# Two transformer blocks on one core: a layer norm inside the second FFN moved behind its matmul, the front reordered, and zero matmuls at two places

## The chip, the cores and the metric

The program runs on one core of one Trainium2 chip, in one launch. The metric is the device time of an execution in microseconds (us). Three runs of the kernel before gave 410.98, 412.43 and 413.91 us, median 412.43.

The names of the engines are those of the profile: PE is TensorE (PEld its weight loads), DVE is VectorE, ACT is ScalarE, POOL is GpSimd, SP is SyncE, which here only issues DMAs. Each engine works through its own list of instructions in order; semaphores tie the lists together.

## The reference

The input x has 4 batches of 256 tokens with 256 features, in float32. Two blocks follow each other; both add an attention and a feed-forward network (FFN) of the same normed input to x:

```python
x = L0_attn_seq
xn = _layernorm(x, axis=-1)
x = x + _L0_attn_ref(xn, ...) + _L0_ffn_ref(xn, ...)
xn = _layernorm(x, axis=-1)
x = x + _L1_attn_ref(xn, ...) + _L1_ffn_ref(xn, ...)
```

The first attention reshapes its input into many sequences of only two tokens; a causal mask lets a token see so little that the attention comes down to a choice between two learned memory entries. The first FFN is one ternary matrix 256 by 256. The second attention has 32 query heads and 4 key/value heads of width 64, rotary position embedding on q and k, and a causal softmax over 256 tokens. The second FFN is the part that the change rebuilds:

```python
def ternarize_weights(w):
    gamma = jnp.mean(jnp.abs(w))
    return jnp.sign(jnp.round(w / (gamma + EPS))) * gamma
def bitlinear(x, w):
    xn = layer_norm(x)
    ...
    return jnp.einsum('bsd,od->bso', x_hat, w_hat)
h = bitlinear(x, w_fc)                    # 256 -> 1024
h = jax.nn.gelu(h, approximate=False)
return bitlinear(h, w_proj)               # 1024 -> 256, with a layer norm of h inside
```

## The kernel before, in words

Everything is written out by hand: one function for each engine (`@block.tensor`, `@block.vector`, and so on) holds that engine's list in program order, and every wait is explicit. Products in nearly full float32 accuracy are made by splitting a matrix into a high part and a low part ("hi", made by ACT or DVE while rounding, and "lo", the difference, made by DVE or POOL) and adding the matmuls of the parts.

**The front.** SP issues the loads from HBM. PE multiplies the memory entries with the first attention's weights (`g_products` L972, `m_products` L980, four pieces each), transposes the normed tokens y0 (L962), forms the scores of the first attention (L1010) into one bank, DVE and ACT turn them into shares of two (`small`, L754 to L767), and PE multiplies (`ffn_0` L1029, `attention_0` L1036). DVE adds the result to x for one batch after another (`add0` L783), takes the statistics of the next norm (`stats1`), asks POOL for the square root (POOL raises to the power -0.5, `root` L574), writes the normed tokens y1 (`norm1` L323, called `y` in the trace), and PE transposes them (`turn_tokens`), from which ACT makes xT_hi (L465) and DVE xT_lo (L812). The ternary weights are made on DVE in three passes over each matrix (`ternary`, L735 to L737).

**The second FFN** runs in 8 tiles of 128 tokens, in STEPS that PE walks at L1267 and the others beside it. For a tile t: `fc` (L1081, PE), `gelu` (L484, ACT), `hidden_stats` (L826 to L832, DVE), a root on POOL, `hidden_factors` (L836, L837, DVE), `hidden_y` (L497, ACT, one pass over 1024 columns that applies the inner layer norm), `hidden_T` (L962, PE, two halves of four transposes), `hidden_hi` (L491, ACT), `hidden_lo` (L841, DVE), `proj` (L1109, PE, 16 matmuls), `ffn_add` (L846, DVE). Tile t is transposed and multiplied three and four steps after its `fc`.

**Fills and blocks.** Between these steps PE projects q, k and v of the second attention ("fills", L1139 and L1155). A fill of q or k is a block n = 0, 1, 2, ...; five fills are prepared in the front (k of batch 0, q of group 0 in two halves, v of batch 0, first half of q of group 1). ACT copies a block out of PSUM (`raw`, L477), SP moves its halves with four DMAs (`turned`, L359 and L360), POOL multiplies and adds the rotary embedding in five passes (L621, L623, L631, L632, L633), and SP moves the result into qT with four DMAs or kT with eight (L380, L383). `raw` and `turned` have two buffers: ACT may copy block n only when POOL is through with `rope_products` of block n-2, and waits for that in its list. POOL also makes the low parts of the weights of q and of the output (L588), two after each of the first blocks, 18 units in all.

**The second attention** is 16 pairs (batch, group) of 6 units, so 96 slots n. In slot n PE computes the scores (L1191, mask L1194), transposes the probabilities of slot n-2 (L962), multiplies with v (L1228) and projects out (L1248); DVE and ACT do the softmax. The fills go on in the slots: in an iteration (6 slots) the second half of q of the next pair at unit 0, the first half of q of the pair after it at unit 3, and at units 4 k or v of the next batch. The first half of a pair's q is needed at its unit 0, the second half at its unit 3. So block 9, the second half of q of pair 3, is projected in slot 12 and needed in slot 21.

## Time and profile before

| | |
|---|---|
| Median of three runs | 412.43 us |
| Profiled execution, time of it | 411.61 us |
| Profiled execution, span | 409.8 us |
| PE busy | 369.4 us, 90% of the span |
| DVE, ACT, POOL busy | 310.9, 251.9, 272.2 us |
| HBM read | 13.14 MB |

The profiled execution's own time is 1.8 us above its span, and 0.8 us below the median. The profile's strip of 40 slices (10.2 us each) shows PE at nine tenths or more from slice 13 to the last but one; all its holes lie in the first 12 slices, the front. POOL is at nine tenths in slices 14 to 18, and mostly lower later. In the kernel's timelines idle time stands in brackets behind an instruction, with the instruction that ended it.

### The profile page before, as it was taken

The page shows a single profiled execution, that of the slowest core. Times are in us where ns is not written, and L with a number is a line of the kernel's source. Part 1 is how long each engine was busy: PE and PEld are TensorE (multiplying, and loading weights), DVE is VectorE, ACT ScalarE, POOL GpSimd, SP SyncE. Part 2 cuts the span into 40 slices and gives each one's busy share as a digit, 9 for nine tenths or more (in the row PEclk, how much of TensorE's full clock was granted, in tenths as well). Part 3 has the DMA queues.
Part 4 walks back from the last instruction along what each step waited for, and adds up shares of the span by engine and source line. Part 5 has one row for each costly group of instructions (what it writes and reads, how often), then busy time and mean ns, then how long its engine had stood idle before and what let it go on. Part 6 is the DMA issues. An engine that isn't in the chain of part 4 may idle for free.

```text
span 409.8 us, 8388 instructions
## 1 busy us (share of the span) xinstructions
PE 369.4 (90%) x2860; PEld 344.7 (84%) x2860; DVE 310.9 (76%) x693; ACT 251.9 (61%) x803; POOL 272.2 (66%) x225
## 2 busy tenths in 40 slices
PE   3968593399889999999999999999999999999995
PEld 1645582379879999999999999999999999998985
DVE  3776786876768777877877788787778778787883
ACT  1142354267768877575767767586776767677671
POOL 3350437346597999998776989767698886777000
PEclk9986798599999999999999999999999999999999
...
GB/s 262 417 417 189 0 26 27 103 26 53 78 78 41 115 97 87 136 130 97 99 108 86 101 168 119 92 95 111 87 104 166 118 95 90 111 80 93 78 0 27
DMA packets 34219, 45.15 MB, mean 110 GB/s; under 512 B 5505, under 2 KB 25986, under 8 KB 33794
## 3 DMA queue, kind: packets, MB, share of 16 engines
...
q14 instruction: 18, 0.15, 0.1%
q10 hardware_dynamic: 146, 0.00, 0.0%
HBM read 13.14 MB, written 1.05 MB: 35 GB/s over the span
## 4 chain that ended last, share of the span: by engine, by line
PE 78%; DVE 9%; ACT 6%; POOL 2%; issue 2%; DMA 2%; SPq 0%; DVEq 0%; POOLq 0%
PE bank L1228 17%; PE bank L1191 13%; PE bank L962 12%; PE bank L1139 12%; PE bank L1248 11%; PE bank L1194 3%; PE bank L1109 2%; DMA wq0T<-in_L_attn_w_qkv_dram 2%; PE bank L980 2%; PE bank L1155 1%; PE bank L972 1%; PE bank L1081 1%; DVE hT_lo L841 1%; POOL qkvT_lo L588 1%; DVE y L323 1%
## 5 line engine op out<-in xcount | busy, mean ns | idle before, releaser
L507 ACT ACTIVATE bank<-bank,neg_max 128x256 f32<-128x256 f32 (+1 forms) x256 | 101.2, 396 | 6.7 <-DVE neg_max L869 6.6
L516 ACT ACTIVATE probT_hi<-bank 128x512 fp32r<-128x512 f32 x96 | 57.5, 599 | 73.3 <-PE bank L962 73.1
L869 DVE TENSOR_REDUCE neg_max<-bank 128x2 f32<-128x512 f32 (+1 forms) x96 | 66.0, 687 | 32.5 <-PE bank L1194 32.4
L1228 PE MATMUL bank<-probT_hi,v 128*128 128x256 f32 x384 | 76.6, 296 | 0.5 <-DVE oT_lo L897 0.5
L623 POOL TENSOR_TENSOR rope_b<-turned,cst 128x512 f32<-128x512 f32 x36 | 46.7, 1297 | 40.0 <-DMA turned<-raw 39.8
L1191 PE MATMUL bank<-kT,qT 128*128 128x256 f32 (+1 forms) x512 | 73.2, 275 | 0.0
L885 DVE TENSOR_TENSOR prob<-bank,rsum 128x512 f32<-128x512 f32 x96 | 66.3, 691 | 3.3
L1191 PEld LDWEIGHTS bank<-kT,qT 128*128 128x128 f32 x512 | 66.6, 192 | 0.0
L891 DVE TENSOR_TENSOR probT_lo<-bank,probT_hi 128x512 fp32r<-128x512 f32 x96 | 65.2, 680 | 0.5 <-ACT probT_hi L516 0.4
L1228 PEld LDWEIGHTS bank<-probT_hi,v 128*128 128x128 f32 x384 | 58.8, 190 | 3.2 <-issue 1.9
L962 PE MATMUL bank<-cst,prob 128*128 128x128 f32 x384 | 57.8, 273 | 1.4 <-DVE prob L885 1.4
L1228 PE MATMUL bank<-probT_lo,v 128*128 128x256 f32 x192 | 54.1, 282 | 0.0
L507 ACT ACTIVATION_READ_ACCUMULATOR bank<-bank,neg_max 128x1 f32 x256 | 53.6, 209 | 0.0
L962 PEld LDWEIGHTS bank<-cst,prob 128*128 128x128 f32 x384 | 45.9, 141 | 4.2 <-DVE prob L885 1.8
L633 POOL TENSOR_TENSOR split_lo<-rope_a,split_hi 128x512 fp32r<-128x512 f32 x36 | 46.2, 1285 | 2.8
L631 POOL TENSOR_TENSOR split_hi<-rope_a,rope_b 128x512 fp32r<-128x512 f32 x36 | 46.3, 1286 | 2.5
L621 POOL TENSOR_TENSOR rope_a<-raw,cst 128x512 f32<-128x512 f32 x36 | 46.9, 1302 | 0.0
L632 POOL TENSOR_TENSOR rope_a<-rope_a,rope_b 128x512 f32<-128x512 f32 x36 | 46.5, 1291 | 0.0
L897 DVE TENSOR_TENSOR oT_lo<-bank,oT_hi 128x256 fp32r<-128x256 f32 x64 | 27.1, 424 | 18.4 <-ACT oT_hi L521 18.1
L1228 PEld LDWEIGHTS bank<-probT_lo,v 128*128 128x128 f32 x192 | 36.5, 190 | 0.0
L1139 PE MATMUL bank<-xT_hi,qkvT_hi 128*128 128x256 f32 x144 | 30.8, 295 | 0.0
L1194 PE MATMUL bank<-mask_b,ident_b 128*128 128x256 bf16 (+1 forms) x96 | 30.6, 318 | 0.0
...
## 6 DMA issues: line engine op xcount, KB each, us to landing
...
qT<-split_hi SPq DMA_DIRECT2D x64, 128.0 KB, 2.4
qT<-split_lo SPq DMA_DIRECT2D x64, 128.0 KB, 2.4
...
kT<-split_hi SPq DMA_DIRECT2D x16, 128.0 KB, 2.4
```

Of the source, the lines that this page charges most:

```text
L507: ins = nc.scalar.activation(own, own, ACT.Exp, bias=neg_max[it % 2][:, first + j:first + j + 1], accum_out=sums[it % 2][:, first + j:firs ...
L516: nc.scalar.activation(probT[0][:, n % 4, :], bank[2 + n % 2][:, :], ACT.Copy).then_inc(t_hi, 1)
L621: pool.tensor_tensor(a, whole, cos, ALU.mult)
L623: own_done(pool.tensor_tensor(z, half, sin, ALU.mult))
L632: own_done(pool.tensor_tensor(a, a, z, ALU.add))
L869: dve.tensor_reduce(neg_max[n // UNITS % 2][:, unit_columns(n % UNITS)], score_bank(n)[:, :].rearrange("p (h k) -> p h k", h=heads), AX.X, ...
L885: dve.tensor_tensor(a, e, share, ALU.mult).then_inc(s_norm, 1)
L891: dve.tensor_tensor(lo, bank[2 + n % 2][:, :], hi.bitcast(F32), ALU.subtract).then_inc(t_lo, 1)
L962: ins = pe.transpose(ps[:, P * j:P * j + P], a, ident)
L1139: ins = pe.matmul(bank[place][:, SEQ * j:SEQ * j + SEQ], qkvT[w][:, k, at:at + P], xT[s][:, k, SEQ * b:SEQ * b + SEQ], start=i == 0, stop= ...
L1191: pe.matmul(ps[:, keys * j:keys * j + keys], qT[it % 2][:, h + j, P * c:P * c + P], kT[b % 2][:, g, s, 0:keys], start=j == 0 and s == 0, s ...
L1228: ins = pe.matmul(group_bank(), v[b % 2][:, DH * z:DH * z + P], p, start=m == 0, stop=m == last)
```

## The change

The names keep their meaning; line numbers in the diff's headers are left out.

- **The inner norm is deferred.** `hidden_y` is gone. PE transposes the gelu's output as it is, and `proj` multiplies it. `ffn_add` multiplies the product by the tile's factor while it adds (one DVE instruction as before). The mean's part, mean times factor times the column sums of the weights, is added on POOL: `mean_part`, two instructions of 128x256 a tile, placed after the weights' low parts that follow blocks 4 to 11. The column sums are eight matmuls on PE in step 5 (`column_sums`), copied out by ACT. `add_out` waits for the mean parts.
- **The pipeline is shorter.** Tile t is transposed one step after its `fc` and multiplied two steps after. STEPS falls from 12 to 10, and slots 0 and 1 alone are placed in the steps. All fills go to bank 6, the hidden transposes to banks 4 and 7. Fill k of batch 0 now waits until all four batches are added to x.
- **Ternary weights** take one pass on DVE (`rounded`) and one on ACT (`sign`).
- **y1** is written by ACT (`normal1`), with a bias for which POOL makes one more small product after each root.
- **The front's order.** The load of the constants goes behind x, that of w_fc ahead of `wout`. PE transposes y0 before the first `m_products`; the first score product's work on DVE no longer stands behind the sum over w_fc and the four casts of xT_hi; the constants' casts go from DVE to POOL.
- **Zero matmuls.** PE multiplies a zeroed bf16 tile 14 times into bank 5 at its start and 8 times into bank 4 ahead of `turn_tokens(0)`, 512 columns each; nothing reads the result.

```diff
-        SLOTS_AT = {8: (0,), 9: (1,), 10: (2,), 11: (3,)}
+        WCOL_STEP = 5
+        SLOTS_AT = {8: (0,), 9: (1,)}
         FILL = ([f for step in sorted(FILLS_IN) for f in FILLS_IN[step]]
                 + [f for it in range(ITS) for u in range(UNITS) for f in fills_at(it, u)])
         PREPARED = sum(map(len, FILLS_IN.values()))
...
+                    sp.dma_start(cst[:, 0:C_QC], const[:, 0:C_QC]).then_inc(ld["cst"], 16)
             sp.dma_start(nat_ffn0[:, :, :], w_ffn0).then_inc(ld["ffn0"], 16)
+            sp.dma_start(nat_fc[:, :, :], w_fc).then_inc(ld["fc"], 16)
             for i in range(WQ0_PIECES):
                 own = slice(piece * i, piece * i + piece)
                 sp.dma_start(wout0[:, own, :], w_out0[:, own, :]).then_inc(ld_wout[i], 16)
-            sp.dma_start(nat_fc[:, :, :], w_fc).then_inc(ld["fc"], 16)
...
+            def sign(n, w, out, done):
+
+                act.wait_ge(tern_in, n + 1)
+                nc.scalar.activation(out, w, ACT.Sign, bias=neg_magic[:, 0:1]).then_inc(done, 1)
...
-            for b in range(B):
-                whole_x(b)
+            whole_x(0)
+            whole_x(1)
+            whole_x(2)
             act.wait_ge(e_in, 1)
             nc.scalar.activation(small[:, 1, :], small[:, 0, :], ACT.Exp).then_inc(e_out, 1)
+            whole_x(3)
+            sign(0, nat_ffn0[:, :, :], ffn0T[:, :, :], tern0)
...
+            sign(1, nat_fc[:, :, :], fcT[:, :, :], tern_fc)
...
+                act.wait_ge(nb_done, b + 1)
+                for t in (2 * b, 2 * b + 1):
+                    ins = nc.scalar.activation(y1[:, b, t % 2, :], x[:, b, t % 2, :], ACT.Identity, bias=tok[:, 3, t:t + 1],
+                                               scale=tok[:, 0, t:t + 1])
+                ins.then_inc(y1_done, 1)
...
+            normal1(0)
             tokens_hi(0)
+            normal1(1)
             done = 3
             for step in range(STEPS):
-                hidden_hi(step - 3, 0)
-                if 0 <= step - 2 < TILES:
-                    hidden_y(step - 2)
-                hidden_hi(step - 3, 1)
+                hidden_hi(step - 1, 0)
+                hidden_hi(step - 1, 1)
                 if step < TILES:
                     gelu(step)
+                if step < B - 1:
+                    tokens_hi(step + 1)
+                empty(FILLS_IN.get(step, ()))
+                if step < B - 2:
+                    normal1(step + 2)
+                if step == 1:
+                    sign(2, nat_proj[:, :, :], projT[:, :, :], tern_proj)
                 if step == TILES - 1:
                     nc.scalar.activation(table_use[:, 0:1], table_use[:, 1:2], ACT.Exp)
-                if step in (0, 2, 3):
...
+                own = slice(2 * b, 2 * b + 2)
+                root(tok[:, 0:2, own], b + 3)
+                pool.wait_ge(root_out, b + 3)
+                pool.tensor_tensor(tok[:, 3, own], tok[:, 3, own], tok[:, 0, own], ALU.mult).then_inc(nb_done, 1)
...
+            def mean_part(t):
+
+                if t == 0:
+                    pool.wait_ge(wcol_done, 1)
+                pool.wait_ge(f_add, t + 1)
+                pool.tensor_tensor(mcol[:, :], wcol[:, :], ffac[:, t, 4:5].to_broadcast([P, DIM]), ALU.mult).then_inc(mean_made, 1)
+                pool.wait_ge(mean_made, t + 1)
+                part = x[:, t // 2, t % 2, :]
+                pool.tensor_tensor(part, part, mcol[:, :], ALU.add).then_inc(f_mean, 1)
+                pool.wait_ge(f_mean, t + 1)
...
+                if n - 4 < TILES:
+                    mean_part(n - 4)
...
-            def ternary(w, out, inverse):
-
-                link(dve.tensor_scalar(w, w, inverse, 1.0, ALU.mult, ALU.min))
-                link(dve.tensor_scalar(w, w, -1.0, MAGIC, ALU.max, ALU.add))
-                return dve.tensor_scalar(out, w, -MAGIC, None, ALU.add)
...
+            def rounded(w, inverse):
+
+                dve.tensor_scalar(w, w, inverse, MAGIC, ALU.mult, ALU.add).then_inc(tern_in, 1)
...
+            def high_part(b):
+
+                dve.wait_ge(full_done, b + 1)
+                dve.tensor_copy(xT[0][:, :, SEQ * b:SEQ * b + SEQ],
+                                yT_full[:, b, :].rearrange("p (k t) -> p k t", k=KC)).then_inc(x_hi, 1)
+
+            dve.wait_ge(sum_out, 2)
+            link(dve.tensor_scalar(winv[:, 0:1], bank[5][:, 0:1], 1.0 / (DIM * DIM), 1e-5, ALU.mult, ALU.add))
+            link(dve.reciprocal(winv[:, 0:1], winv[:, 0:1]))
+            rounded(nat_ffn0[:, :, :], winv[:, 0:1])
+            high_part(0)
...
+            for b in range(1, B):
+                high_part(b)
...
-            normal1(0)
             stats1(1)
+            hidden_scale(0)
             tokens_lo(0)
+            dve.wait_ge(sum_out, 3)
+            weight_scale(2, bank[3][:, 0:1]).then_inc(scaled, 1)
+            dve.wait_ge(scaled, 1)
...
             def ffn_add(t):
                 dve.wait_ge(f_out, t + 1)
-                dve.tensor_tensor(x[:, t // 2, t % 2, :], x[:, t // 2, t % 2, :], bank[5][:, 0:DIM],
-                                  ALU.add).then_inc(f_add, 1)
+                part = x[:, t // 2, t % 2, :]
+                dve.scalar_tensor_tensor(part, bank[5][:, 0:DIM], ffac[:, t, 3:4], part, ALU.mult, ALU.add).then_inc(f_add, 1)
...
+                dve.wait_ge(f_mean, 2 * b + 2)
...
-            weight_scale(2, bank[3][:, 0:1]).then_inc(scaled, 1)
             add0(2)
-            normal1(1)
             stats1(2)
+            tokens_lo(1)
             add0(3)
-            tokens_lo(1)
+            stats1(3)
+            rounded(nat_proj[:, :, :], winv[:, 2:3])
+            hidden_scale(1)
             for step in range(1, STEPS):
-                t = step - 3
-                if 0 <= t < TILES:
+                t = step - 1
+                if t < TILES:
+                    hidden_stats(t)
                     hidden_lo(t, 0)
-                if step <= TILES:
...
-                    normal1(3)
-                    ternary(nat_proj[:, :, :], projT[:, :, :], winv[:, 2:3]).then_inc(tern_proj, 1)
-                if step == 3:
-                    tokens_lo(3)
-                if 0 <= t < TILES:
                     hidden_lo(t, 1)
...
+
+                for _ in range(count):
+                    pe.matmul(bank[b][:, :], idle_in[:, 0:P], idle_in[:, :], start=True, stop=True)
+
+            pe.wait_ge(idle_ready, 1)
+            keep_busy(5, 14)
             pe.wait_ge(blk_done, 1)
             for i in range(WQ0_PIECES):
                 g_products(i)
-            m_products(0)
             for b in range(B):
...
-            m_products(1)
-            sum_up(0, bank[5][:, 0:1])
+            m_products(0)
             pe.wait_ge(g_done, 1)
...
+            sum_up(0, bank[5][:, 0:1])
+            sum_up(1, bank[5][:, 1:2])
+            m_products(1)
             m_products(2)
-            sum_up(1, bank[5][:, 1:2])
...
-            ffn_0(0)
             pe.wait_ge(prob0, 1)
             for b in range(B):
                 ins = pe.transpose(bank[4][0:2 * H, P * b:P * b + P], small[:, 3, 2 * H * b:2 * H * b + 2 * H], ident)
             ins.then_inc(p0_T, 1)
             m_products(3)
+            ffn_0(0)
             ffn_0(1)
...
             ffn_0(2)
             attention_0(2)
             sum_up(2, bank[3][:, 0:1])
+            keep_busy(4, 8)
             turn_tokens(0)
...
-                pe.wait_ge(f_y, t + 1)
...
+                pe.wait_ge(f_gelu, t + 1)
+                if t:
                     pe.wait_ge(f_lo, 2 * t + half - 1)
...
+            def column_sums():
+
+                emptied(pe, ("v", 0))
+                pe.wait_ge(tern_proj, 1)
+                pe.wait_ge(ones_done, 1)
+                for c in range(FF // P):
+                    ins = pe.matmul(bank[6][:, 0:DIM], ones_r[:, :], projT[:, c, :], start=c == 0, stop=c == FF // P - 1)
+                ins.then_inc(wcol_full, 1)
...
                 if f == ("k", 0):
-                    pe.wait_ge(y1_lo, 1)
-                if f == ("q", 0, 0):
                     pe.wait_ge(o0_added, B)
+                if f == ("q", 0, 1):
+                    pe.wait_ge(y1_lo, B)
+                if f == ("q", 1, 0):
+                    pe.wait_ge(wcol_done, 1)
...
-                t = step - 3
+                t = step - 1
                 if 0 <= t < TILES:
                     hidden_T(t, 0)
+                    hidden_T(t, 1)
                 if step < TILES:
                     fc(step)
-                if 0 <= t < TILES:
-                    hidden_T(t, 1)
+                if step < B - 1:
+                    turn_tokens(step + 1)
                 if t >= 1:
                     proj(t - 1)
-                if step in (0, 2, 3):
-                    turn_tokens(max(step, 1))
                 fill(FILLS_IN.get(step, ()))
+                if step == WCOL_STEP:
+                    column_sums()
```

What the change moves is seen in three places. On DVE early in the front, from the scale of w_ffn (`winv`) to the shares of the first attention (`small`), before:

```order
L735 TENSOR_SCALAR nat_ffn_107<-nat_ffn_107,winv 128x512
L736 TENSOR_SCALAR nat_ffn_107<-nat_ffn_107 128x512
L737 TENSOR_SCALAR ffn0T<-nat_ffn_107 128x512
L745 CAST xT_hi<-yT_full 128x2x256 x4
L748 TENSOR_REDUCE wsum<-nat_fc 128x1
L754 TENSOR_SCALAR small<-bank,tok 128x64 x4
L759 TENSOR_TENSOR small<-small 128x128
L761 TENSOR_TENSOR small<-small 128x128 x2
L764 TENSOR_TENSOR small<-small 128x128
L765 RECIPROCAL small<-small 128x128
L767 TENSOR_TENSOR small<-small 128x128 x2
```

and now:

```order
L788 TENSOR_TENSOR small<-small 128x128 x2
L798 TENSOR_SCALAR winv<-bank 128x1
L799 RECIPROCAL winv<-winv 128x1
L775 TENSOR_SCALAR nat_ffn_107<-nat_ffn_107,winv 128x512
L794 CAST xT_hi<-yT_full 128x2x256
L803 TENSOR_TENSOR small<-small 128x128
L804 RECIPROCAL small<-small 128x128
L806 TENSOR_TENSOR small<-small 128x128 x2
L794 CAST xT_hi<-yT_full 128x2x256 x3
L813 TENSOR_SCALAR wscale<-bank 128x1
L814 TENSOR_SCALAR winv<-wscale 128x1
```

The two further passes over `nat_ffn`, three of the four casts and the sum over `nat_fc` no longer stand ahead of `small`'s last instructions.

On DVE around the second tile's factors, before (`y` is the normed token of batch 3, `nat_proj` the ternary passes):

```order
L836 TENSOR_SCALAR ffac<-ffac,wscale 128x1
L837 TENSOR_SCALAR ffac<-ffac,fmv 128x1
L812 TENSOR_TENSOR xT_lo<-bank,xT_hi 128x256 x2
L323 TENSOR_SCALAR y_64<-x,mv,tok 128x256 x2
L801 RECIPROCAL tok<-tok 128x2
L802 TENSOR_TENSOR tok<-tok 128x2
L803 TENSOR_TENSOR tok<-tok 128x2
L804 TENSOR_SCALAR ffac<-tok,wscale 128x2
L735 TENSOR_SCALAR nat_proj<-nat_proj,winv 128x2048
L736 TENSOR_SCALAR nat_proj<-nat_proj 128x2048
L737 TENSOR_SCALAR projT<-nat_proj 128x2048
L841 TENSOR_TENSOR hT_lo<-bank,hT_hi 128x512
```

and now, for the first tile:

```order
L871 BN_AGGR fmv<-fstat 128x2
L720 TENSOR_SCALAR ffac<-fmv 128x1
L874 RECIPROCAL ffac<-fmv 128x1
L875 TENSOR_TENSOR ffac<-ffac,fmv 128x1
L884 TENSOR_TENSOR hT_lo<-bank,hT_hi 128x512 x2
L879 TENSOR_SCALAR ffac<-ffac,wscale 128x1
L880 TENSOR_SCALAR ffac<-ffac,fmv 128x1
L852 TENSOR_TENSOR xT_lo<-bank,xT_hi 128x256 x2
```

The low parts hT_lo of a tile now stand ahead of its factors L879, which wait for POOL's root; before, the first hT_lo stood behind the second tile's factors, the norm and the three passes.

On POOL from the weights' low parts after block 3, before:

```order
L588 TENSOR_TENSOR woT_lo<-nat_o,woT_hi 128x512
L621 TENSOR_TENSOR rope_a<-raw,cst 128x512
L623 TENSOR_TENSOR rope_b<-turned,cst 128x512
L631 TENSOR_TENSOR split_hi<-rope_a,rope_b 128x512
L632 TENSOR_TENSOR rope_a<-rope_a,rope_b 128x512
L633 TENSOR_TENSOR split_lo<-rope_a,split_hi 128x512
L588 TENSOR_TENSOR qkvT_lo<-nat_qkv,qkvT_hi 128x2x256
L588 TENSOR_TENSOR woT_lo<-nat_o,woT_hi 128x512
L621 TENSOR_TENSOR rope_a<-raw,cst 128x512
L623 TENSOR_TENSOR rope_b<-turned,cst 128x512
```

and now:

```order
L608 TENSOR_TENSOR woT_lo<-nat_o,woT_hi 128x512
L649 TENSOR_TENSOR rope_a<-raw,cst 128x512
L651 TENSOR_TENSOR rope_b<-turned,cst 128x512
L659 TENSOR_TENSOR split_hi<-rope_a,rope_b 128x512
L660 TENSOR_TENSOR rope_a<-rope_a,rope_b 128x512
L661 TENSOR_TENSOR split_lo<-rope_a,split_hi 128x512
L608 TENSOR_TENSOR qkvT_lo<-nat_qkv,qkvT_hi 128x2x256
L608 TENSOR_TENSOR woT_lo<-nat_o,woT_hi 128x512
L672 TENSOR_TENSOR mcol<-wcol,ffac 128x256
L675 TENSOR_TENSOR x<-x,mcol 128x256
L649 TENSOR_TENSOR rope_a<-raw,cst 128x512
L651 TENSOR_TENSOR rope_b<-turned,cst 128x512
```

Between two blocks there now stand two more instructions, the mean's part L672 and L675; this happens eight times.

## Rows read from the trace of the kernel before

**Rows 1.** Waits of PE, first 124.4 us: who waited for whom, us, times, longest.

```profile
PE bank L962 <- DVE hT_lo L841: 15.8, 6, 13.2
...
PE bank L962 <- DVE y L323: 4.8, 1, 4.8
...
PE bank L990 <- DVE wsum L748: 3.9, 1, 3.9
...
PE bank L972 <- DMA wq0T<-in_L_attn_w_qkv_dram: 7.3, 2, 7.0
```

**Rows 2.** Windows by stage: us, busy (x instructions) of each engine, granted clock, DMA share, GB/s.

```profile
78.00:124.40 46.40, 42.52 (x297) 38.72 (x298) 31.41 (x82) 31.63 (x61) 31.94 (x29) 0.94 0.25 58
...
124.40:172.30 47.90, 47.44 (x400) 46.15 (x400) 38.19 (x77) 35.58 (x123) 44.45 (x37) 1.00 0.41 97
...
172.30:409.80 237.50, 232.03 (x1940) 224.82 (x1938) 185.97 (x375) 159.43 (x571) 165.73 (x131) 1.00 0.41 98
```

**Rows 3.** Chain of waits, first 130 us: start us, us, what.

```profile
16.65 1.73 PE bank L980 x8
...
28.18 2.20 DVE wsum L748
...
34.35 1.06 PE bank L1052 x4
...
39.43 1.89 ACT abs_out L443 x2
...
41.34 1.28 ACT L533
...
43.43 2.49 POOL qkvT_lo L588 x2
...
45.92 0.98 POOL tok L574
```

**Rows 4.** Timeline of DVE: start us, us, instruction, [idle before, releaser].

```profile
41.07 0.69 DVE L783 TENSOR_TENSOR x<-x,bank 128x512 f32<-128x512 f32 x1 [2.48 <-PE bank L1036]
...
43.46 1.27 DVE L679 TENSOR_SCALAR tok<-tok 128x2 f32<-128x2 f32 x1
...
68.98 0.27 DVE L836 TENSOR_SCALAR ffac<-ffac,wscale 128x1 f32<-128x1 f32 x1 [3.17 <-POOL ffac L574]
...
70.08 2.74 DVE L323 TENSOR_SCALAR y<-x,mv,tok 128x256 f32<-128x256 f32 x2
```

**Rows 5.** Window of one of PE's waits.

```profile
43.80:48.60 4.80, 0.03 (x1) 0.00 (x0) 3.19 (x5) 0.60 (x2) 4.32 (x4) 0.70 0.00 0
```

**Rows 6.** Chain of waits, one tile of the hidden FFN and a fill.

```profile
94.69 0.63 PE bank L962 x4
...
99.53 1.46 PE bank L1139 x12
```

**Rows 7.** Timeline of POOL, the stage that follows.

```profile
111.94 1.27 POOL L631 TENSOR_TENSOR split_hi<-rope_a,rope_b 128x512 fp32r<-128x512 f32 x1
...
132.40 1.27 POOL L623 TENSOR_TENSOR rope_b<-turned,cst 128x512 f32<-128x512 f32 x1 [2.58 <-DMA turned<-raw]
...
172.30 1.29 POOL L621 TENSOR_TENSOR rope_a<-raw,cst 128x512 f32<-128x512 f32 x1
```

**Rows 8.** Timeline of ACT, block 5's copy out of PSUM.

```profile
127.81 0.62 ACT L477 ACTIVATE raw<-bank 128x512 f32<-128x512 f32 x1
```

**Rows 9.** POOL's groups by form: xcount, busy us, mean ns, idle before.

```profile
L633 POOL TENSOR_TENSOR split_lo<-rope_a,split_hi 128x512 fp32r<-128x512 f32 x36 | 46.2, 1285 | 2.8
...
L574 POOL TENSOR_TENSOR ffac<-ffac,neg_half 128x1 f32<-128x1 f32 x8 | 4.4, 550 | 19.6 <-DVE ffac L679 19.5
```

**Rows 10.** Timeline of SP's queue, block 9's last move.

```profile
175.03 0.61 SPq L380 DMA_DIRECT2D qT<-split_lo  x1
```

**Rows 11.** The page's DMA issues: KB each, median us from issue to landing.

```profile
qT<-split_lo SPq DMA_DIRECT2D x64, 128.0 KB, 2.4
```

**Rows 12.** Timeline of PE, scores of slot 21.

```profile
178.30 1.01 PE L1191 MATMUL bank<-kT,qT 128*128 128x128 f32 x8
```

125 lines of the change are left out of this document (53 added, 72 removed).

## Prediction

> **What bounds the kernel now.** I read the strip of 40 slices first: PE is at nine tenths from slice 13 on, with its holes in the front. PE's waits over the first 124.4 us come next: 13.2 us in one wait for hT_lo, 4.8 for y1, 3.9 for the sum over w_fc, 7.0 for the first weights [rows 1]. The windows by stage show the rest: from 124.4 us on PE is busy 279.5 of 285.4 us, at full clock [rows 2]. So from slot 3 on the kernel is PE's work; the change adds nothing to it there, and it can gain only by letting slot 3 start earlier. But the same windows show a second engine near its limit: POOL is busy 44.45 of the 47.9 us from 124.4 to 172.3. It stays behind its blocks there, and the change gives it more to do.
>
> **The front, replayed.** Times are the trace's, with durations of the same instructions.
>
> 1. PE's g products still end near 16.65 us, since the load of their second piece ends PE's wait. The y0 transposes then start at once; before, the first m products, 1.73 us, stood ahead [rows 3]. Transposes (2.3), one m piece (1.9) and the score product (1.9) put the scores at 22.8.
> 2. DVE before began `small` at 30.38, behind the sum over w_fc, though the scores were there at 24.6. From that to the shares on PE took 34.35-30.38 = 3.97 us [rows 3]. Now it starts at 22.8 with 0.85 us put in (scale, one pass, one cast): 27.6. Then the shares' transposes (0.53, half of the row's 1.06 at the lower clock), the m products (1.8), ffn_0 twice (0.95 each) and an attention product (0.87): the first add at 32.9 instead of 41.07 [rows 4], 8 us earlier.
> 3. ACT takes some of it back. The one pass over w_fc ends at 32.1; sign (1.9, priced like the pass L443 over the same 2048 columns), |w_proj| (2.1) and the table load (1.5) follow, then the first high part. POOL's first low part starts at 38.2 instead of 43.43. Behind it come low parts 2.49, root 0.98 [rows 3], the new small product (0.1 to 0.5, I take 0.3, by the nearest small POOL rows) and two norms on ACT (0.95): y1 is turned at 43.1 instead of 48.65, 5.5 us earlier.
> 4. The 8 zero matmuls ahead of it take 1.7 us while PE waits; PE is still idle for 4.9 us from 38.2 to 43.1. In the wait of 4.8 us before, the granted clock fell to a mean of 0.70 within the window, so to its lower level (1.2 GHz) [rows 5]. I let it fall again and price the pair of stretches alike. The 14 at the start lie inside PE's 7.0 us wait for weights: no cost, no gain, since the next piece is waited for anyway.
> 5. fc(0) starts at 47.0. Fill k now waits for all four adds, behind `tokens_lo(1)`: 52.4. PE idles 3.0 us there, a new wait. The second tile's transposes come at 59.7, proj(0) at 63.0 (before 86.1).
> 6. The 13.2 us wait arose on DVE: factors of tile 1 waited 3.17 us for POOL's root, then came the norm of batch 3 (2.74) and three ternary passes, 3.8 us, all ahead of hT_lo [rows 4]. POOL's root still stands behind a block's products, and DVE still waits for it, until 67.3; but both hT_lo of the tile now stand ahead. Only ffn_add(0) is late, and proj(1) with it: 1.5 us, at 69.5.
> 7. From there PE has no wait longer than a few tenths. A tile (two halves, fc, proj) takes 99.53-94.69 = 4.84 us, 0.19 of it from a start behind a wait, so 4.65; a fill 1.46 [rows 6]. Column sums are 8 matmuls of 0.12, 0.95 us, paid in full. Fill v ends at 79.0; two tiles, the sums and a fill later, q of block 3 ends at 79.0+9.3+0.95+1.46 = 90.7 (before 100.99).
> 8. Two tiles, two slots and the fill of slot 0 follow; proj(7) ends at 102.2, and slot 3 starts near 104.8 instead of 124.4. **PE alone would gain 19.6 us.** ACT loses eight `hidden_y` of 1.2 us and DVE nearly all it did in pairs of passes; neither ends a wait after step 7, so no term.
>
> **POOL's list, from block 3 on.** Block 3's copy is there at 91.4; a copy's halves land about 4.6 us after it (block 5: copy at 127.81, L623 released at 132.40 [rows 7, 8]). So L623 runs at 95.9, the last tile's root follows, 0.55 us [rows 9], and L631 starts at 97.8 instead of 111.94. From L631 to the end of block 9 the list took 172.30-111.94 = 60.4 us before, 2.58 of them a wait for a landing that does not come back, since POOL is further behind: 57.8. New are five mean pairs ahead of that point. No row shows such an instruction. A product of 128x512 takes 1.285 us, so 256 columns cost at least 0.64 and at most 1.29; I take 0.72, half and a little for the fixed part, that is 1.5 a pair with its own two waits. The bounds are 1.3 and 2.6 a pair. Five pairs are 7.5 us, and block 4's halves cost 0.3: 97.8+57.8+7.5+0.3 = 163.4.
>
> [...]
>
> Block 9's last move was issued at 175.03, 2.7 us after the block's end, and landed 2.4 us later [rows 10, 11]: 177.4; slot 21, which needs it, began at 178.30 [rows 12]. So before, this hand-over had 0.9 us to spare. Now it lands at 163.4+5.1 = 168.5, while PE would be ready at 158.7. **Slot 21 starts 9.8 us earlier, not 19.6.** The other 9.8 us show as waits on PE between slots 12 and 21: ACT's copy of block 9 stands behind POOL's products of block 7, and then the scores. After slot 21 the blocks have more slack (three more pairs, 4.5 us, against 2.5, 5 and 7 us of spare at blocks 10 to 12), and PE's work sets the end.
>
> **Sum:** 411.61-9.8 = 401.8 us for the profiled execution; the median of the runs lies 0.8 above it, so 402.6. I say **402**. The pair's bounds give 400.8 to 407.3; each us by which block 3 comes earlier or later is one us.
>
> **A second rule against it.** A `tensor_scalar` on DVE of two columns took 1.27 us from 43.46 on, beside a POOL instruction from 43.43 on; others of its kind take 0.17 [rows 3, 4]. The factors L836, one column wide, took 0.27 and do not show this. The Trainium skill (SBUF, section on the two separate sides) has DVE and GpSimd share a port pair that one holds for its whole instruction, the other fully blocked. By that rule DVE's two-column steps and the pass over w_proj each wait up to 1.3 us, and block 3 comes later; it is priced in the third case.
>
> **The cases.**
>
> - *POOL sets slot 21* (chance 0.48): 402, its own range 398 to 406. For it: the 0.9 us of spare; against it: block 3's time is a long replay.
> - *POOL binds little* (0.12): if block 3 comes several us earlier and pairs cost 1.3, the time goes towards PE's own bound, 411.6-19.6 = 392; I put it at 394. Against it: POOL's 44.45 of 47.9 us.
> - *The front gives less* (0.22): DVE's steps wait for POOL instructions (five of them, 6.5 us at most), or roots come a block later, or the clock falls again in the 3.0 us wait of point 5. Block 3 is then 4 to 6 us later: 406 to 408.
> - *The change doesn't do what it says* (0.12): the hole only moves, as DVE and POOL wait for each other's roots in every step. For it: PE's longest wait came from such a knot. Then block 3 moves 4 us at most: 408 to 415.
> - *Slower* (0.06): the mean pairs on POOL. It decides from 3.5 us a pair, where five of them eat 9.8 us; a broadcast factor that doubles a full-width instruction, 2.6 us each and 5.2 a pair, gives 402+5x3.7 = 420.
>
> The last two hold 0.18; the others reach from 393 to 409, my range. A measurement here can tell about 1% (4 us) from no change. Faster by over 1% is the first two and most of the third, 0.78; within 1% 0.15; slower 0.07.
>
> **What the profile after will show.** The first add near 33; y1 turned near 43 with a clock at the lower level; no wait of PE for hT_lo over 2 us; hT_lo's L884 ahead of L879; block 3's L659 near 98 and slot 3 near 105. From there POOL without a gap to about 163, mean instructions of 0.7 us, ACT waiting for POOL at block 9's copy, and PE waiting for a qT landing at slot 21. The forecast fails if POOL has gaps there (time towards 392) or the pairs are long, or if block 3 is not within 3 us of 98.

## The result

The changed kernel takes 407.9 us (median of six runs, 407.06 to 409.41), the kernel before 411.7 us on the same chip (six runs, 410.35 to 413.91). The ratio is 0.9904, with a 95% interval from 0.9875 to 0.9934: a little faster, 3.8 us by the medians. The forecast was 402. The profiled execution has a span of 407.1 us and a time of 408.87 us. Its page shows less work on DVE (303.8 us for 310.9) and more on POOL (285.9 for 272.2). PE is busy for 7.1 us more than before; 6.6 us of it are the zero matmuls:

```profile
PE 376.5 (92%) x2873; PEld 350.5 (86%) x2890; DVE 303.8 (75%) x676; ACT 251.1 (62%) x808; POOL 285.9 (70%) x250
```

The longest waits of PE over the whole span (who waited for whom, us, times, longest). The wait of 13.2 us for hT_lo and that of 3.9 for the sum over w_fc [rows 1] are gone, and of the 7.3 us for the first weights 2.7 are left. The 4.8 us for y1 are as long as before. Four waits of 2.5 to 3.7 us are new: for x (twice, L890 and L824), for qT and for probT_lo.

```profile
PE bank L994 <- ACT y L474: 4.8, 1, 4.8
PE bank L1148 <- DVE x L890: 3.7, 1, 3.7
PE bank L1239 <- DMA qT<-split_lo: 2.9, 1, 2.9
PE bank L1189 <- DVE x L824: 2.9, 1, 2.9
PE bank L1003 <- DMA wq0T<-in_L_attn_w_qkv_dram: 2.7, 1, 2.7
PE bank L1276 <- DVE probT_lo L934: 2.5, 1, 2.5
```

**The front until step 2** came nearly as replayed. The rows are from the chain of waits (start us, us, what) and answer to [rows 3]. y1 is turned at 43.67 us where the prediction has 43.1.

```profile
10.64 7.08 PE bank L1003 x24
...
38.76 2.49 POOL qkvT_lo L608 x2
...
43.67 1.11 PE bank L994 x4
...
73.07 3.61 PE bank L1148 x16
```

The last of these rows is the first that is far off: proj(1) starts at 73.07 instead of 69.5 and takes 3.61 us instead of 1.9. What it waited for is in DVE's timeline (start, us, instruction, [idle before, releaser]), the answer to [rows 4]:

```profile
68.75 0.27 DVE L879 TENSOR_SCALAR ffac<-ffac,wscale 128x1 f32<-128x1 f32 x1 [2.64 <-POOL ffac L594]
...
70.04 1.15 DVE L843 TENSOR_TENSOR tok<-tok 128x2 f32<-128x2 f32 x1
71.23 1.30 DVE L844 SCALAR_TENSOR_TENSOR ffac<-tok,wscale 128x2 f32<-128x2 f32 x1
72.45 0.47 DVE L890 SCALAR_TENSOR_TENSOR x<-bank,ffac,x 128x256 f32<-128x256 f32 x1
```

and in POOL's over the same stretch:

```profile
64.31 1.30 POOL L608 TENSOR_TENSOR qkvT_lo<-nat_qkv,qkvT_hi 128x512 fp32r<-128x512 f32 x1 [4.54 <-ACT qkvT_hi L464]
65.56 1.27 POOL L649 TENSOR_TENSOR rope_a<-raw,cst 128x512 f32<-128x512 f32 x1
66.79 1.29 POOL L651 TENSOR_TENSOR rope_b<-turned,cst 128x512 f32<-128x512 f32 x1
68.16 0.55 POOL L594 TENSOR_TENSOR ffac<-ffac,neg_half 128x1 f32<-128x1 f32 x1
...
69.92 1.26 POOL L660 TENSOR_TENSOR rope_a<-rope_a,rope_b 128x512 f32<-128x512 f32 x1
71.25 1.26 POOL L661 TENSOR_TENSOR split_lo<-rope_a,split_hi 128x512 fp32r<-128x512 f32 x1
```

Read them together. DVE had the input of tile 1's root ready at 63.9 us. POOL, idle for 4.54 us, was waiting for ACT's high part of a weight, and the two products of rope block 0 stood behind that in its list, so the root ran at 68.16. Then DVE's L843 and L844, two columns each, took 1.15 and 1.30 us instead of 0.16 and 0.22: L843 ends at 71.19, where POOL's L660 ends, and L844 at 72.53, where L661 ends.

**From block 3 on** (POOL's timeline; the rows answer to [rows 7]) the anchor is 103.34 us, not 97.8:

```profile
103.34 1.29 POOL L659 TENSOR_TENSOR split_hi<-rope_a,rope_b 128x512 fp32r<-128x512 f32 x1
...
167.21 1.27 POOL L661 TENSOR_TENSOR split_lo<-rope_a,split_hi 128x512 fp32r<-128x512 f32 x1
```

POOL has no gap between them. Its list there took 168.5-103.3 = 65.1 us (predicted: 65.6). The mean parts by form (xcount, busy us, mean ns, idle before):

```profile
L675 POOL TENSOR_TENSOR x<-x,mcol 128x256 f32<-128x256 f32 x8 | 5.9, 736 | 0.6
...
L672 POOL TENSOR_TENSOR mcol<-wcol,ffac 128x256 f32<-128x256 f32 x8 | 4.9, 614 | 0.0
```

The wait of PE that the prediction had between slots 12 and 21 is there too. ACT may copy block 9 only when POOL is through with the products of block 7 (L651 at 143.63, 1.27 us); it waits 4.93 us for them, and the softmax work behind it in ACT's list comes late, so that PE waits 2.47 us for probT_lo at 146.86:

```profile
144.99 0.60 ACT L495 ACTIVATE raw<-bank 128x512 f32<-128x512 f32 x1 [4.93 <-POOL rope_b L651]
```

Slot 21 follows on PE, where [rows 12] had 178.30 and 1.01 us for the same eight matmuls, and the window behind it (columns as in [rows 2]) shows a mean granted clock of 0.58:

```profile
172.90 1.97 PE L1239 MATMUL bank<-kT,qT 128*128 128x128 f32 x8 [2.95 <-DMA qT<-split_lo]
```

```profile
172.00:180.00 8.00, 7.10 (x37) 6.85 (x38) 2.68 (x5) 2.69 (x11) 7.69 (x8) 0.58 0.43 101
```

So slot 21 begins 5.4 us earlier than before, and from there to the end it takes 407.1-172.9 = 234.2 us instead of 409.8-178.3 = 231.5. What is left of the 5.4 is 2.7 us of span.

### The profile page after: what moved, and what is told of

It is laid out like the page before. It is cut to its first block, busy times and chain, and to the rows that moved or that the text cites. A ratio compares the mean times of both kernels' runs of the same rounds, so it can differ in the third digit from the quotient of the medians.

```text
span 407.1 us, 8459 instructions
## 1 busy us (share of the span) xinstructions
PE 376.5 (92%) x2873; PEld 350.5 (86%) x2890; DVE 303.8 (75%) x676; ACT 251.1 (62%) x808; POOL 285.9 (70%) x250
## 4 chain that ended last, share of the span: by engine, by line
PE 66%; POOL 18%; DVE 6%; ACT 3%; issue 3%; DMA 3%; SPq 1%; POOLq 0%
PE bank L1276 14%; PE bank L1239 11%; PE bank L994 10%; PE bank L1296 10%; PE bank L1189 9%; PE bank L1148 3%; POOL woT_lo L608 2%; PE bank L1124 2%; POOL split_lo L661 2%; POOL split_hi L659 2%; POOL rope_b L651 2%; POOL rope_a L660 2%; POOL qkvT_lo L608 2%; PE bank L1242 2%; POOL rope_a L649 2%
## 5 line engine op out<-in xcount | busy, mean ns | idle before, releaser
L1239 PE MATMUL bank<-kT,qT 128*128 128x256 f32 (+1 forms) x512 | 75.2, 281 | 2.9 <-DMA qT<-split_lo 2.9
L651 POOL TENSOR_TENSOR rope_b<-turned,cst 128x512 f32<-128x512 f32 x36 | 46.4, 1290 | 36.9 <-DMA turned<-raw 36.9
L1239 PEld LDWEIGHTS bank<-kT,qT 128*128 128x128 f32 x512 | 68.4, 196 | 3.1 <-DMA qT<-split_lo 3.1
L994 PE MATMUL bank<-cst,prob 128*128 128x128 f32 x384 | 58.7, 276 | 3.1 <-DVE prob L928 2.1
L661 POOL TENSOR_TENSOR split_lo<-rope_a,split_hi 128x512 fp32r<-128x512 f32 x36 | 46.3, 1285 | 2.8
L660 POOL TENSOR_TENSOR rope_a<-rope_a,rope_b 128x512 f32<-128x512 f32 x36 | 46.4, 1290 | 0.0
L495 ACT ACTIVATE raw<-bank 128x512 f32<-128x512 f32 x36 | 21.8, 606 | 28.6 <-PE bank L1189 20.8
L1276 PEld LDWEIGHTS bank<-probT_lo,v 128*128 128x128 f32 x192 | 36.4, 190 | 0.0
```

Source lines behind the costliest of these rows:

```text
L651: own_done(pool.tensor_tensor(z, half, sin, ALU.mult))
L660: own_done(pool.tensor_tensor(a, a, z, ALU.add))
L994: ins = pe.transpose(ps[:, P * j:P * j + P], a, ident)
L1239: pe.matmul(ps[:, keys * j:keys * j + keys], qT[it % 2][:, h + j, P * c:P * c + P], kT[b % 2][:, g, s, 0:keys], start=j == 0 and s == 0, s ...
L1276: ins = pe.matmul(group_bank(), v[b % 2][:, DH * z:DH * z + P], p, start=m == 0, stop=m == last)
```

## The experiments

**The theory** after the traces: the prediction's mechanism holds, and two of its sizes failed: block 3's anchor, for what follows from tile 1's late root (DVE's two steps beside POOL's instructions, and the clock behind PE's wait), and the clock behind slot 21's wait, which had no term. **Rivals:** the zero matmuls cost the time; the front's lateness is absorbed later and something else sets slot 21. Each row gives the ratio to the kernel before on the same chip. The runs e1 to e4, e5 to e8, e9 to e12 and e13 to e15 were each made on one chip, on which the kernel before had a median of 412.68, 411.04, 411.88 and 412.08 us; medians of different groups carry these differences, the ratios do not.

| Kernel | median, us | ratio, 95% interval |
|---|---|---|
| the change | 407.9 | 0.990 (0.988 to 0.993) |
| e1 without the 14 zero matmuls | 408.77 | 0.989 (0.983 to 0.995) |
| e2 without the 8 | 407.25 | 0.987 (0.983 to 0.991) |
| e3 ffn_add first | 407.46 | 0.987 (0.983 to 0.992) |
| e4 means late | 399.55 | 0.969 (0.965 to 0.972) |
| e5 matmuls in slot 21's wait | 406.05 | 0.985 (0.981 to 0.989) |
| e6 means late, root early | 394.87 | 0.958 (0.954 to 0.962) |
| e7 = e6, ffn_add first | 394.33 | 0.958 (0.953 to 0.963) |
| e8 = e4 without zero matmuls | 400.50 | 0.971 (0.967 to 0.975) |
| e9 root early | 403.54 | 0.980 (0.977 to 0.982) |
| e10 = e9, matmuls in slot 21's wait | 401.49 | 0.976 (0.973 to 0.979) |
| e11 = e7, last root late | 396.69 | 0.962 (0.959 to 0.965) |
| e12 hidden_scale by columns | 408.37 | 0.990 (0.986 to 0.993) |
| e13 = e6, 26 zero matmuls for 8 | 394.72 | 0.958 (0.954 to 0.961) |
| e14 = e13, 10 more in g's wait | 392.36 | 0.953 (0.950 to 0.957) |
| e15 = e9 without mean parts | 394.72 | 0.958 (0.955 to 0.962) |

### The zero matmuls: e1, e2, e8

```diff
-            keep_busy(5, 14)      # e1, e8
-            keep_busy(4, 8)       # e2, e8
```

> The changed kernel without the 14 matmuls of zeros ahead of g_products (place 1); all else stays. Theory A (they lower the clock later: the profile after has 2.67 us of waiting for the second piece of wq0 and a granted clock of 0.72 in 11 to 17 us, with them gone piece 0 is slow and hides that wait): the last product of g ends at 16.6 to 16.9 instead of 17.72 us, first add at about 33 instead of 34.00, and since PE and ACT lead the front the block 3 sums on POOL (L659) come about 1 us earlier, 102.3; end 406 to 407 us. Theory B (they keep the clock up and are worth something): g ends later than 17.7, time 408.5 or more. Theory C (a later wait absorbs 1 us of the front): g ends earlier, L659 of block 3 stays at 103.4 and the time at 407.9 within 0.5.

> The changed kernel without the 8 matmuls of zeros ahead of turn_tokens(0) (place 2). Theory A (they fill only 1.6 of the 4.8 us in which PE waits for y1 and don't stop the clock, which stood at 0.59 in 45 to 50 us with them): ffn_0(3) and fc(0) take the same 1.7 and 2.3 us within 0.3, time within 0.5 us of the changed kernel's 407.9. Theory B (without them the clock falls further or sooner): fc(0) takes 3 us or more and the time is over 409.

> Base: the kernel with the mean parts late (399.55 us, its six runs within 1.6 us of each other). Here without any of the 22 matmuls of zeros. Theory A (they cost and gain nothing): 399.5 within 0.7. Theory B (they keep the clock up somewhere): 400.5 or more, with a lower granted clock in 11 to 17 or in 45 to 60 us. Theory C (they cost): 398.5 or less.

None of the three can be told from its base by its time (e8 is 0.95 us above e4 by the medians, and the intervals overlap). The 14 did shorten what stands right behind them: the first eight g products took 1.94 us with them and 3.64 us without (e1). It gained nothing, because PE waits for the next piece of the weights anyway: the next product began at 10.64 and 10.79 us. The g products behind PE's wait for weights took 5.39 us in e1 and 6.90 in e8, both without zero matmuls there, and with the 14 they took 5.39 in e2 and 7.08 in the change's profile.

The longer form in the change goes with the length of the wait ahead of it. In the four profiles with waits of 2.58 to 2.67 us (the change, e5, e9, e13) the 24 products took 7.08 us, at a granted clock of 0.72 in 11 to 17 us; in the nine others with the 14 and without matmuls in this wait, with waits of 1.63 to 2.46 us, they took 5.39, at 1.00. e8's 6.90 is another form: there each product lasts 0.63 us in the trace from the first at 5.41 on until about 13.2, and 0.38 behind that, although the granted clock's column says 1.00. Theory A of e1 held in the trace, where the wait is shorter (1.93 us) and the products end at 16.2 us instead of 17.7, but not in the time. The first line is e1's, the second e8's:

```profile
10.79 5.39 PE L1003 MATMUL bank<-wq0T,blk_k 128*64 128x256 f32 x24 [1.93 <-DMA wq0T<-in_L_attn_w_qkv_dram]
```

```profile
10.58 6.90 PE L1003 MATMUL bank<-wq0T,blk_k 128*64 128x256 f32 x24 [1.53 <-DMA wq0T<-in_L_attn_w_qkv_dram]
```

### ffn_add first: e3

```diff
                     hidden_lo(t, 1)
+                if t >= 1:
+                    ffn_add(t - 1)
+                if t < TILES:
                     hidden_factors(t)
...
-                if t >= 1:
-                    ffn_add(t - 1)
```

> The changed kernel with ffn_add(t-1) on VectorE ahead of hidden_factors(t) (and so ahead of tokens_lo and hidden_scale) in each step; in the profile after, TensorE waited 3.69 us for ffn_add(0) at 72.45, behind a wait for GpSimd's root till 68.75 and two 2-column instructions of 1.15 and 1.30 us. Theory A (this wait and the lower clock behind it made the front late): ffn_add(0) starts at 66.2 to 66.8, proj(1) at once after turn_tokens(3) (about 69.4) at full clock in 1.9 us, the block 3 sums (L659) about 3 to 5 us earlier than 103.37, slot 21 as much earlier than 172.90, time 402.5 to 405. Theory B (the front is led by ScalarE's weights or by GpSimd from there on and waits later instead): proj(1) is early, but L659 of block 3 within 1 us of 103.4, time 407 to 408.5.

ffn_add(0) came at 63.95 us and proj(1) without a wait, but the wait moved on by one instruction, to hidden_T(2), because DVE still stood behind the root and its small steps when hT_lo was due:

```profile
73.32 1.04 PE L995 MATMUL bank<-cst,ffn_h 128*128 128x128 f32 x5 [2.68 <-DVE hT_lo L884]
```

Block 3's sums start at 100.90 us, but those of e2, which does nothing in this place, at 101.19: most of the 2.4 us is front that ran at full clock in this profile. The time did not move: the order on DVE alone is not what costs. The root stands behind both orders; e6 and e9 move it.

### The mean parts late: e4

```diff
-                if n - 4 < TILES:
-                    mean_part(n - 4)
+                if 0 <= n - 10 < TILES:
+                    mean_part(n - 10)
```

> The changed kernel with the eight mean parts on GpSimd after rope blocks 10 to 17 instead of 4 to 11. Theory A (GpSimd's list sets slot 21, five pairs of 1.47 us stand in it): block 9's last sum ends about 7.3 us earlier than 168.5, slot 21 is ready before TensorE, whose own pace is then the bound (some 2.9 us of waiting go, and the low clock behind them, 2.7 us), the waits of the mean parts move to where GpSimd is ahead; 402 to 403.5 us. Theory B (TensorE's wait moves to the next blocks, 10 to 13, since the means still stand ahead of them): a gain of at most 2 us, 406 to 408. Theory C (the means don't bind; slot 21 waits for something else): slot 21 stays at 172.9, 407.9 within 0.5.

Theory A, and more than it said: 399.55 us. The anchor is at 102.80, 0.5 us earlier than in the change. Block 9's last sum ends 57.7 us later (the prediction's 57.8 for a list without means) and slot 21 begins 7.0 us earlier than in the change, at full clock:

```profile
159.24 1.29 POOL L661 TENSOR_TENSOR split_lo<-rope_a,split_hi 128x512 fp32r<-128x512 f32 x1
```

```profile
165.90 1.11 PE L1239 MATMUL bank<-kT,qT 128*128 128x128 f32 x8 [1.54 <-DMA qT<-split_lo]
```

From there to the end of the span it is 397.4-165.9 = 231.5 us, what it was before the change. Without the five pairs the list is 65.1-57.7 = 7.4 us shorter, 1.48 us a pair. PE still waits for qT, but 1.54 us instead of 2.95, and behind this wait the granted clock stays at 1.00 (164 to 180 us).

### Matmuls in slot 21's wait: e5

```diff
+                if n == 21:
+                    pe.wait_ge(s_norm, n - 2)
+                    for _ in range(14):
+                        pe.matmul(score_bank(n)[:, :], ident_b[:, :], mask_b[:, :, :],
+                                  start=True, stop=True, skip_group_check=True)
```

> The changed kernel with 14 more 128x512 bf16 matmuls on TensorE ahead of scores(21), into the score bank that scores(21) then overwrites; they fill the 2.95 us in which TensorE waited for qT (14 by 0.213 us). Theory A (the low clock after that wait, 0.50 in 172.9 to 176 us and 0.65 in 176 to 180 us, cost 2.7 us): the granted clock stays at 1.00 from slot 21 on, slot 21 starts within 0.3 us of where it would, and from its start to the end of the span it takes 231.5 to 232 us as before the change, instead of 234.2; the time falls by 2 to 2.7 us from the changed kernel. Theory B (the low clock comes from something else, or what it costs is absorbed by waits later): less than 0.7 us.

This profile has the change's front to 0.2 us, so the two can be laid side by side. PE's wait is filled with 3.20 us of matmuls, slot 21 starts at 172.65 us (172.90), and the window that showed a clock of 0.58 now shows 1.00:

```profile
169.52 3.20 PE L1228 MATMUL bank<-mask_b,ident_b 128*128 128x512 bf16 x14
```

```profile
172.00:180.00 8.00, 8.00 (x64) 7.10 (x63) 5.31 (x12) 4.88 (x18) 7.69 (x8) 1.00 0.43 100
```

From slot 21 to the end it takes 404.1-172.65 = 231.5 us again. The low clock cost 2.7 us in this pair of profiles. By the medians it is 1.85 us, on two chips; the intervals of the two ratios overlap a little. e9 and e10 below are a second pair.

### The root early: e6, e7, e9, e10

```diff
             tile_root(0)
+            tile_root(1)
             weights_lo(4, 5)
             ...
             rope_products(0)
-            tile_root(1)
```

> The changed kernel with GpSimd's tile_root(1) ahead of weights_lo(4,5) and rope block 0, the mean parts where the change put them. This is the state that the prediction worked from (ffn_add(0) at 69.5 us, block 3's sums at 97.8). Theory A (the anchor was the first error of the sum, and from it the list runs as predicted): L659 of block 3 at 97.5 to 98.5, block 9's last sum ends 65.1 later at 162.6 to 163.6, slot 21 starts at 167.0 to 168.0, and from there to the end 231.5 to 234.2; the time is 400.5 to 404, nearest 402.5. Theory B (TensorE's wait at slot 21 grows by what the front gains, since GpSimd is the bound and is fed by something else): 405 to 408.

> The changed kernel with tile_root(1) early and 14 matmuls ahead of scores(21). Alone the 14 matmuls gave 1.85 us by the medians and 3.0 us of span between two profiles with the same front. Theory A (anchor and clock are the two errors of the sum, and they add): 1.8 to 3 us under the kernel with the early root alone, 398.5 to 401. Theory B (the wait at slot 21 is another one once the front is early): within 0.7 us of it.

e9 brings block 3's sums near the predicted time and leaves all behind them as it was: they start at 98.76 us (predicted 97.8), block 9's last sum ends at 163.9 (163.4), and slot 21 starts at 168.35 (168.5).

```profile
98.76 1.29 POOL L659 TENSOR_TENSOR split_hi<-rope_a,rope_b 128x512 fp32r<-128x512 f32 x1
...
162.62 1.27 POOL L661 TENSOR_TENSOR split_lo<-rope_a,split_hi 128x512 fp32r<-128x512 f32 x1
```

```profile
168.35 1.97 PE L1239 MATMUL bank<-kT,qT 128*128 128x128 f32 x8 [3.00 <-DMA qT<-split_lo]
```

The time is 403.54 us against 407.9. Behind the wait of 3.00 us the rest takes 402.9-168.35 = 234.55 us, so the clock's term is there again, and e10, which fills that wait, takes it out: slot 21 starts at 167.63 us, and the rest takes 399.2-167.63 = 231.6 us.

```profile
167.63 1.19 PE L1243 MATMUL bank<-kT,qT 128*128 128x128 f32 x8
```

The median is 401.49, 2.05 us less, with intervals that overlap a little. This is near the forecast's 402, but e9 is not the schedule that the prediction replayed. The replay had DVE waiting for the root until 67.3 us; in e9 DVE does not wait for it at all, and two steps that the replay had at full speed still wait for POOL, 1.4 us together (L843 0.45 us, L844 1.33). What e9 saves on the one makes up for the other, so that block 3 comes near the predicted time:

```profile
65.82 0.26 DVE L879 TENSOR_SCALAR ffac<-ffac,wscale 128x1 f32<-128x1 f32 x1
...
68.08 1.33 DVE L844 SCALAR_TENSOR_TENSOR ffac<-tok,wscale 128x2 f32<-128x2 f32 x1
```

> Base: the kernel with the mean parts late (399.55 us). Here GpSimd's tile_root(1) also stands ahead of weights_lo(4,5) and of the products of rope block 0, behind which VectorE waited for it 2.6 us. Theory A (that root led the front): hidden_factors(1) at 64.5 to 65 instead of 68.2, ffn_add(0) at 66.5 to 69 instead of 71.9, TensorE's wait of 3.7 us before proj(1) down to 1 or less, block 3's sums (L659) 1.5 to 3 us earlier than 102.80, slot 21's wait of 1.54 gone: 397 to 398.5 us. Theory B (the two-column instructions on VectorE that wait for GpSimd, or ScalarE's weights, hold the front anyway): L659 within 1 us, time within 0.7 of 399.5.

> Base: the mean parts late and tile_root(1) early; in addition ffn_add(t-1) on VectorE ahead of hidden_factors(t). With ffn_add alone moved, the wait of 3.7 us went from proj(1) to hidden_T(2) (2.68 us, for hT_lo behind the same root). Theory A (root and add together take the wait away): no wait over 1.5 us on TensorE in 60 to 80 us, block 3's sums at 98.5 to 100.5, slot 21 without a wait for qT, 396.5 to 398 us. Theory B (the front's time is then set by ScalarE or by the low clock): no gain over the kernel with the early root alone, within 0.5 us.

With the means late as well (e6) the two add up: 394.87 us, 4.7 less than e4 (e9 gave 4.4). ffn_add(0) is at 68.19, block 3's sums at 97.62, and the granted clock in 70 to 80 us is 1.00 instead of 0.83, which the expectation did not have; its 397 to 398.5 us was too high. L844 still waits for a POOL instruction:

```profile
64.66 0.27 DVE L879 TENSOR_SCALAR ffac<-ffac,wscale 128x1 f32<-128x1 f32 x1
...
66.95 1.33 DVE L844 SCALAR_TENSOR_TENSOR ffac<-tok,wscale 128x2 f32<-128x2 f32 x1
68.19 0.47 DVE L890 SCALAR_TENSOR_TENSOR x<-bank,ffac,x 128x256 f32<-128x256 f32 x1
```

Moving ffn_add too (e7) adds nothing that can be measured; its theory A was wrong on the time.

### The last root late: e11

```diff
-            tile_root(7)
             rope_sums(3)
+            tile_root(7)
```

> Candidate for the best version: mean parts late, tile_root(1) early, ffn_add first, and tile_root(7) behind rope_sums(3) instead of ahead of it. Theory A (the list from block 3 on sets slot 21, TensorE waits 1.6 to 2.2 us there): block 3's sums start 0.6 to 1.0 us earlier (96.4 to 96.8), slot 21's wait is as much shorter, 393.3 to 394.0 against 394.3 to 394.9. Theory B (ffn_add(7) and what waits for it, project_out(0) and bank 5, become late by the root's 2.3 us): 395 to 397.

Theory B's side, by the trace (396.69 us against e7's 394.33, with intervals that overlap): block 3's sums start 1.1 us earlier than in e7 (96.25), but DVE waits 1.43 us for the root, the slots' first maxima come behind it, ACT copies block 4 at 102.77 instead of 100.69, and POOL then stands still for the landing. The list is 1.1 us later, and PE's wait at slot 21 grows to 2.72 us.

```profile
107.32 1.29 POOL L651 TENSOR_TENSOR rope_b<-turned,cst 128x512 f32<-128x512 f32 x1 [1.71 <-DMA turned<-raw]
```

### hidden_scale by columns: e12

```diff
-                link(dve.tensor_tensor(f1[:, own], f1[:, own], ms[:, own], ALU.mult))
+                for t in (2 * b, 2 * b + 1):
+                    ins = dve.tensor_tensor(f1[:, t:t + 1], f1[:, t:t + 1], ms[:, t:t + 1], ALU.mult)
+                link(ins)
```

and the next instruction in the same way.

> The changed kernel with the two instructions of hidden_scale (128x2, all operands in SBUF) issued per column, as four of 128x1. In the profile after, these took 1.15 and 1.30 us in step 2, each beside a GpSimd instruction of 1.26 to 1.29 us, against 0.16 and 0.22 where GpSimd was idle. Theory A (the form of more than one column has to wait for GpSimd's instruction, the single column has not): the four take about 0.2 us each, ffn_add(0) starts about 1.5 to 1.9 us earlier than 72.45, time 405 to 407. Theory B (any form with two SBUF operands waits): one or more of the four takes over 1 us, time 407.5 to 409.

Theory B. One column waits as two did; in each of the two rows of DVE one instruction of the two took the long time (L847: 0.21 and 1.24 us). DVE's rows, then POOL's:

```profile
68.31 1.22 DVE L844 TENSOR_TENSOR tok<-tok 128x1 f32<-128x1 f32 x2
69.57 1.36 DVE L847 SCALAR_TENSOR_TENSOR ffac<-tok,wscale 128x1 f32<-128x1 f32 x2
```

```profile
68.19 1.26 POOL L660 TENSOR_TENSOR rope_a<-rope_a,rope_b 128x512 f32<-128x512 f32 x1
69.53 1.26 POOL L661 TENSOR_TENSOR split_lo<-rope_a,split_hi 128x512 fp32r<-128x512 f32 x1
```

### More zero matmuls, and no means: e13, e14, e15

```diff
-            keep_busy(4, 8)
+            keep_busy(4, 26)      # e13, e14
...
                 g_products(i)
+                if i == 0:
+                    keep_busy(5, 10)      # e14
```

> Base: the kernel with the mean parts late and tile_root(1) early (394.87 us). Here 26 matmuls of zeros instead of 8 stand ahead of turn_tokens(0), so that TensorE's wait for y1 (1.67 us filled by the 8, 4.83 us left) is filled to the end. Theory A (the zeros of place 2 did nothing because they were too few: the clock fell to 0.70 in 45 to 50 us behind the open wait): the granted clock is 1.00 in 34 to 50 us, ffn_0(3) with its attention takes 1.5 instead of 3.2 us, fc(0) 1.9 instead of 2.9, the k fill is 1.5 to 2.5 us earlier unless it waits for add0(3), and the end comes 0.5 to 2 us earlier. Theory B (the zeros do not hold the clock, whatever their number): low clock as before, 394.9 within 0.7.

> Base: as the kernel with 26 matmuls of zeros at place 2; in addition 10 matmuls of zeros behind the first eight products of g, in the 1.5 to 2.7 us in which TensorE waits for the second piece of w_qkv0. In the profiles so far the 24 products of g behind that wait took 5.39 us in some and 6.90 to 7.08 us in others of kernels that don't differ there. Theory A (the wait is what lets the clock fall): 5.39 us, and over six runs a narrower spread at the fast end, 0.3 to 1.5 us under the kernel without them. Theory B (the extra matmuls load TensorE more and the throttle comes anyway or elsewhere, or delay the products): same or up to 1 us slower.

> The changed kernel with tile_root(1) early and without the eight mean parts on GpSimd: the mean's share of the second FFN's output is left out. It bounds what the mean parts cost. Theory A (late they are free, since GpSimd is bound only up to slot 21): the same as the kernel with the means late and the root early, 394.9 within 0.7. Theory B (late they still cost): 393.5 or less.

With 26 matmuls PE waits 0.96 us for y1 instead of 4.83, and the window from 36 to 50 us is at full clock. The first line is e6's, the second e13's:

```profile
36.00:50.00 14.00, 8.76 (x34) 6.77 (x32) 7.60 (x27) 5.65 (x13) 7.24 (x9) 0.76 0.00 1
```

```profile
36.00:50.00 14.00, 11.48 (x59) 6.89 (x57) 9.10 (x33) 8.29 (x17) 7.05 (x8) 1.00 0.01 3
```

So 26 zero matmuls held the clock across the wait, and eight did not. Yet e13 is not faster than e6. Counted from the end of the g products, PE reaches the k fill 2.7 us earlier (33.7 for 36.4 us); in this profile the long form of those products took 1.6 of it back, and the clock falls now behind the 2.94 us wait at the k fill (0.83 in 50 to 54 us, where e6 has 1.00): block 3's sums start at 97.94 us, where e6 has 97.62. It falls once more behind slot 21's wait of 1.35 us (0.50 in 162 to 164 us). With the wait for weights filled too (e14) the products took 5.39 us and the median is 392.36, the lowest here: five of its six runs have a mean granted clock of 0.996 and times of 391.96 to 392.84, the sixth has 0.991 and 394.89. The interval of its ratio overlaps those of e6 and e13, so its 2.4 us are likely, not shown; the wait ahead of these products is 0.35 us in its profile, and the short form also came in profiles where it was open and up to 2.46 us long. e15 equals e6: late, the mean parts cost nothing that can be measured. e14 is the best version, 4.7% under the kernel before.

## Why the prediction was wrong

- **Steps 1 to 5** held within 1.5 us: first add 34.0 (32.9), y1 turned 43.67 (43.1), k fill 53.89 (52.4) behind a wait of 2.94 us (3.0), proj(0) 63.82 (63.0). The g products ended 1.1 us later than step 1 has it, at 17.7, in their longer form, which is most of the lateness up to there.
- **Step 4** held: the 8 did not stop the clock falling (a mean of 0.76 in 36 to 50 us with them, 0.63 in e2 without), and the 14 neither cost nor gained time by the medians (e1, e8). For the 8 it was their number, not their kind (e13).
- **Step 6 failed**, by its size. It had root, wait and late add in the right order, but took 1.5 us for them. Measured: 3.69 us of waiting before proj(1), of which 2.1 are the two steps that waited for POOL's instructions, and 1.7 more in proj(1) itself, at the lower clock, for which step 6 had no term. So the end of proj(1) is 5.3 us late: 1.4 were there before its wait, 2.2 are the longer wait, 1.7 the clock. At the anchor it is 103.3-97.8 = 5.5 us. The early root takes 4.6 of it back (e9, whose front is the change's to 0.2 us). No run takes out the 2.1 us of the two steps; their price is read from the rows alone. Of the port pair the prediction spoke as of "two-column steps", and priced it only in a case. By the Trainium skill (SBUF — State Buffer, section SBUF: two separate sides) a DVE instruction with two inputs in SBUF, too, and not only one in a mode that uses both ports, contends with a GpSimd instruction that reads SBUF, and the loser blocks for the whole instruction. The rows of L843, L844 and e12's single columns agree. This price belonged in the sum, at the two instructions that stand ahead of an awaited one.
- **Steps 7 and 8** held from where step 6 left them: a tile took 4.64 us (95.72 to 100.36; predicted 4.65), and ffn_add(7), at 107.5 us, is 5.3 later than the 102.2 of proj(7)'s end, as late as the anchor. PE's own 19.6 us were not in reach, as forecast: POOL set slot 21. With the list shorter and the root early (e6) PE is ready for slot 21 at 159.1 us, where the prediction has 158.7.
- **POOL's list** held: 65.1 us for 65.6, a pair at 1.48 for 1.5 (0.61 us for the product with the broadcast factor, 0.74 for the add). PE's slot 21 followed block 9's end by 4.4 us, not 5.1. Theory A of e4, that this list sets slot 21, is the prediction's main claim, and it was shown three ways: e4, e9, e15.
- **A missing term**: the clock behind slot 21's wait. The prediction expected that wait and priced only its length. It cost 2.7 us (e5) and 3.0 (e9 against e10).
- **The sum** with what was measured: slot 21 at 172.9 instead of 168.5, and 2.7 us of clock: 401.8+4.4+2.7 = 408.9; the profiled execution took 408.87. The sum closes by itself, since the 2.7 is what was left over in this profile; what supports it is e5. The median lies 1.0 below the profiled execution, where the prediction put it 0.8 above.
- The third case, the front giving less for DVE's waits on POOL, 406 to 408, is what happened, on top of the first, that POOL sets slot 21. It had a chance of 0.22 although its mechanism was in rows 3 and 4. That its time fits is in part luck: of the 7.1 us above the sum's 401.8, 2.7 are the clock behind slot 21, which the case does not have, and block 3's 5.5 us had shrunk to 4.4 by slot 21.
